# A depthwise convolution as four matmuls on four column groups, fed by four shifted copies made through DRAM

## Chip, core, metric

One Trainium2 chip, one core of it. The metric is the device time of one execution in microseconds (us), as the median of several runs; the profile is of one execution.

## What is computed

A Mamba block and a mixture of experts, both on the layernormed input, both added to it; float32, x of 2 x 2048 rows of 256. What matters here is the convolution of width 4 over time, for each of the 512 inner channels by itself, between a projection and a silu, and the z half beside it:

```python
xn = layernorm(x)
x_in, z = split(xn @ W_in)                    # 512 + 512 columns
conv[d, t] = sum_k conv_w[d, k] * x_in[d, t + k - 3] + conv_b[d]      # zeros ahead of t = 0
u = silu(conv)
dt, B, C = split(u @ W_xproj)                 # 16, 16, 16
delta = softplus(dt @ W_dt + b_dt)
h[t] = exp(delta[t] * A) * h[t-1] + delta[t] * u[t] * B[t]            # 512 channels x 16 states
y[t] = sum_n h[t, n] * C[t, n] + D_skip * u[t]
attn = (y * silu(z)) @ W_out
ffn = sum over the top 2 of 16 experts: w_e * (gelu(layernorm(xn @ W1_e + b1_e)) @ W2_e + b2_e)
out = x + attn + ffn
```

## The kernel before

The 4096 rows are 8 chunks (`c`, `NC`) of 512 time steps. Channels lie on partitions, in four blocks (`dc`) of 128, time along the free axis. A chunk has 64 units (`G = c * 64 + s`, slot `s`), one for each block and state. In a unit ScalarE makes the decay (`exp_unit`, L846, into a ring `hb` of 12), VectorE multiplies du by B (`product`, L1632) and scans (`scan`, L1643), GpSimd multiplies pairs of units by C (`unit_pair`, L658, ring `hc` of 6; for the pairs in `HC_DVE` VectorE does it, `times_c`, L1652), and TensorE adds the states by transposing into `psY` (`sum_unit`, L1150, four units behind).

All else is put between these units by hand-written tables: a table entry names the slot at whose place in an engine's queue the step is issued. `AT` holds for chunks 1 to 6, `AT0` and `AT7` override it for the first and last, `MOE` and `GS` place the twenty groups of the experts, each of four tiles. Each engine walks the same slots; semaphores alone keep them apart. SyncE (SP) issues nearly all loads in the same order, and stands at each wait.

During chunk c, the inputs of chunk c + 1 are made. Every one of these steps passes through one PSUM bank, `psA`, in turn: `project` (two matmuls, L1169), `x_in` (ScalarE copies the bank to `ux`, L780, and three columns for the next chunk's halo, L786), `convolve` (four matmuls of 128 x 128 weights with the diagonal of one tap, `dgw`, on `ux` shifted by the tap, L1177), `x_copy` (bank and bias to `ux`), for dc 3 `x_silu`; then `xd_mm`, `xd_copy`, `d_mm` (L1213), `d_exp`, `d_ln` (`tmpA`, L835) and `d_max` (VectorE, `delta`, L1457). The z half of chunk c takes the same bank in between: `z_mm` (L1225), `z_copy`, `z_silu` (L874 and L876) and, on VectorE, `gate` (L1659). A silu needs another activation table than exp and ln, so `x_silu` and `z_silu` are each followed by a `preload_act_table_set(LNEXP)` (L805, L877), and the compiler puts a load ahead of each activation whose set isn't there.

Ahead of the loop stands a prologue: all rows are normed and transposed (L463, L1324), the router's logits are made on TensorE in four groups of 32 columns (L1339), the routing is worked out on VectorE in one long chain, which needs a matmul over ranks (L1373, behind the convolution of dc 2 in TensorE's queue), and the first chunk's projections, convolutions, x_dbl (L1308) and first delta are made. SP loads x and stores the normed rows and their transpose meanwhile.

## Time and profile before

| | |
|---|---|
| median of 3 runs | 1123.73 us (1122.23 to 1125.07) |
| span of the profiled execution (the only time recorded for it) | 1114.4 us |
| granted TensorE clock, mean | 0.925 |
| busy: VectorE, PE, GpSimd, ScalarE | 1036.3, 930.9, 881.2, 867.0 us |
| moved by DMA | 185.86 MB, 167 GB/s |

The profile's span runs from the first to the last instruction; the median of the runs holds what lies around it as well. PE is TensorE's matmuls, DVE VectorE, ACT ScalarE, POOL GpSimd, SP and SPq SyncE and its queue. L1177 is line 1177 of the kernel.
### The profile page before, as it was taken

The page shows a single profiled execution, that of the slowest core. Times are in us where ns is not written, and L with a number is a line of the kernel's source. Part 1 is how long each engine was busy: PE and PEld are TensorE (multiplying, and loading weights), DVE is VectorE, ACT ScalarE, POOL GpSimd, SP SyncE. Part 2 cuts the span into 40 slices and gives each one's busy share as a digit, 9 for nine tenths or more (in the row PEclk, how much of TensorE's full clock was granted, in tenths as well). Part 3 has the DMA queues.
Part 4 walks back from the last instruction along what each step waited for, and adds up shares of the span by engine and source line. Part 5 has one row for each costly group of instructions (what it writes and reads, how often), then busy time and mean ns, then how long its engine had stood idle before and what let it go on. Part 6 is the DMA issues. An engine that isn't in the chain of part 4 may idle for free.

```text
span 1114.4 us, 16950 instructions
## 1 busy us (share of the span) xinstructions
PE 930.9 (84%) x4575; PEld 630.4 (57%) x4575; DVE 1036.3 (93%) x1304; ACT 867.0 (78%) x1841; POOL 881.2 (79%) x570
## 2 busy tenths in 40 slices
PE   5947766587979999789998999899989999787776
PEld 3424434454656656566666766576656665565564
DVE  7999999799999988997899979999999999899995
ACT  4574788465897799767999699978998798976981
POOL 7178999599777887858787878887897886877995
PEclk9968986698999999899999999799998999899988
DMA  9496568953484544824457553763367443764313
GB/s 328 175 342 227 161 194 290 331 183 92 117 283 153 114 102 143 307 49 95 119 166 278 104 139 75 274 190 72 81 191 266 100 105 92 243 213 114 77 20 66
DMA packets 119367, 185.86 MB, mean 167 GB/s; under 512 B 12012, under 2 KB 104344, under 8 KB 111016
## 3 DMA queue, kind: packets, MB, share of 16 engines
q1 hardware_dynamic: 87120, 144.60, 38.8%
q0 software_dynamic: 19584, 25.26, 13.1%
q10 hardware_dynamic: 12568, 14.93, 4.4%
q8 instruction: 36, 0.59, 0.2%
q14 instruction: 59, 0.48, 0.1%
HBM read 146.34 MB, written 42.60 MB: 170 GB/s over the span
## 4 chain that ended last, share of the span: by engine, by line
PE 36%; issue 16%; ACT 15%; DVE 13%; POOL 11%; DMA 5%; ACTq 2%; SPq 1%; POOLq 0%; DVEq 0%
DVE hb L1643 10%; POOL hc L658 7%; PE psY L1150 7%; PE psA L1177 5%; PE psC L1290 4%; ACT hb L846 4%; PE psC L1240 3%; PE psA L1225 3%; PE psA L1169 2%; PE psE L1267 2%; ACT hnT L967 2%; DVE psB L1632 2%; POOL out L707 2%; DMA Cb<-bc_d 2%; DMA xs_d<-xg,slots 2%
## 5 line engine op out<-in xcount | busy, mean ns | idle before, releaser
L658 POOL TENSOR_TENSOR hc<-hb,Cb 128x1024 f32<-128x1024 f32 x246 | 623.8, 2630 | 83.3 <-PE psY L1150 64.4
L1643 DVE TENSOR_TENSOR_SCAN hb<-hb,carry,psB 128x512 f32<-128x512 f32 x384 | 471.8, 1263 | 7.7 <-ACT hb L846 6.1
L1150 PE MATMUL psY<-ident,hc 128*128 128x128 f32 x2048 | 306.9, 291 | 76.3 <-POOL hc L658 76.2
L846 ACT ACTIVATE hb<-delta,aneg 128x512 f32<-128x512 f32 x512 | 351.5, 716 | 21.7 <-POOL hc L658 15.7
L1150 PEld LDWEIGHTS psY<-ident,hc 128*128 128x128 f32 x2048 | 255.1, 150 | 191.0 <-POOL hc L658 109.4
L1632 DVE TENSOR_TENSOR psB<-Bb,psU 128x512 f32<-128x512 f32 x510 | 323.7, 679 | 0.5 <-DMA Bb<-bc_d 0.5
L707 POOL DMA_INDIRECT out<-yo,idx x80 | 128.0, 1600 | 55.3 <-DMA out<-yo,idx 18.0
L1643 DVE TENSOR_TENSOR_SCAN hb<-hb,psB 128x512 f32<-128x512 f32 x128 | 149.2, 1200 | 2.1 <-ACT hb L846 2.1
L1177 PE MATMUL psA<-ux,dgw 128*128 128x512 f32 x232 | 113.7, 610 | 3.0 <-ACT ux L786 2.0
L1290 PE MATMUL psC<-w2r,hnT 128*128 128x256 f32 x320 | 90.0, 430 | 0.0
L1267 PE MATMUL psE<-w1r,xgT 128*128 128x256 f32 x320 | 82.9, 404 | 0.0
L1290 PEld LDWEIGHTS psC<-w2r,hnT 128*128 128x128 f32 x320 | 63.9, 210 | 18.5 <-issue 10.0
L1267 PEld LDWEIGHTS psE<-w1r,xgT 128*128 128x128 f32 x320 | 59.3, 195 | 16.2 <-issue 9.3
L1169 PE MATMUL psA<-xnT,win 128*128 128x512 f32 x116 | 59.0, 626 | 11.2 <-ACT zs L876 5.0
L967 ACT ACTIVATE hnT<-hnT,vecs 128x128 f32<-128x128 f32 x160 | 64.2, 481 | 1.2 <-issue 0.7
L1225 PE MATMUL psA<-win,xnT 128*128 128x512 f32 x128 | 61.2, 600 | 3.0 <-ACT zs L869 2.2
L1240 PE MATMUL psC<-wout,ygT 128*128 128x256 f32 x248 | 59.8, 383 | 1.2 <-ACT ygT L885 0.8
L1177 PEld LDWEIGHTS psA<-ux,dgw 128*128 128x128 f32 x232 | 41.4, 198 | 31.9 <-issue 26.3
L673 POOL DMA_INDIRECT xs_d<-xg,slots x37 | 40.9, 1104 | 19.2 <-DMA xg<-xn_d 11.4
L1213 PE MATMUL psA<-xr,rows 16*128 16x512 f32 x60 | 40.7, 763 | 15.0 <-DVE delta L1457 14.3
L980 ACT ACTIVATE yo<-psC,wv 128x256 f32<-128x256 f32 x80 | 33.3, 468 | 21.2 <-PE psC L1290 21.2
L666 POOL TENSOR_TENSOR du<-delta,ux 128x512 f32<-128x512 f32 x31 | 44.6, 1438 | 6.6 <-DVE delta L1457 4.4
(235 smaller groups left out, 1205.8 us busy)
## 6 DMA issues: line engine op xcount, KB each, us to landing
Bb<-bc_d SPq DMA_DIRECT2D x32, 1024.0 KB, 6.7
Cb<-bc_d SPq DMA_DIRECT2D x32, 1024.0 KB, 7.5
w1r<-w1c_d SPq DMA_DIRECT2D x80, 256.0 KB, 2.8
w2r<-in_L_ffn_W SPq DMA_DIRECT2D x80, 256.0 KB, 3.5
xg<-xs_d SPq DMA_DIRECT2D x20, 516.0 KB, 5.8
xg<-xn_d SPq DMA_DIRECT2D x37, 128.0 KB, 2.9
Bb<-in_L_attn_x SPq DMA_DIRECT2D x8, 512.0 KB, 7.5
xn_d<-hb SPq DMA_DIRECT2D x8, 512.0 KB, 8.9
```

The source lines that it names most:

```text
L658: pool.tensor_tensor(hc[:, k:k + 2, :], hb[:, g % HR:g % HR + 2, :], Cb[:, n:n + 2, :], ALU.mult).then_inc(s_g, 1)
L707: pool.indirect_dma_start(out=out[:, :], out_offset=bass.IndirectOffsetOnAxis(ap=idx[:, g % 2, j:j + 1], axis=0), in_=yo[:, j, :], in_offs ...
L846: act.activation(hb[:, g % HR, :], delta[:, dc, :], ACT.Exp, scale=aneg[:, dc, n:n + 1]).then_inc(s_exp, 1)
L967: ins = act.activation(hnT[:, j, kc, :], hnT[:, j, kc, :], ACT.Gelu, scale=g1t[:, bass.ds(e, 1), kc], bias=be1t[:, bass.ds(e, 1), kc])
L1150: mm = pe.matmul(y[:, tt * P:(tt + 1) * P], hc[:, g % GR, tt * P:(tt + 1) * P], ident[:, :], start=False, stop=(n == NS - 1), is_transpose ...
L1177: mm = pe.matmul(bank[:, :], dgw[:, dc, k, :], x_of(p, dc)[:, k:k + T], start=(k == 0), stop=(k == KW - 1))
L1225: mm = pe.matmul(psA[:, :], xnT[:, c % 2, kc, tt * P:(tt + 1) * P], win[:, 1, kc, :], start=(kc == 0), stop=(kc == KC - 1))
L1240: mm = pe.matmul(psC[:, 0:D], ygT[:, dc, :], wout[:, dc, :], start=(dc == 0), stop=(dc == dc_out(c) - 1))
L1267: mm = pe.matmul(psE[:, a * D:(a + 1) * D], xgT[:, a, kc, :], w1r[:, a, kc, :], start=False, stop=(kc == KC - 1), skip_group_check=True)
L1290: mm = pe.matmul(psC[:, a * D:(a + 1) * D], hnT[:, 2 * h + a, kc, :], w2r[:, 2 * h + a, kc, :], start=False, stop=(kc == KC - 1), skip_gro ...
L1632: dve.tensor_tensor(psB[g % 2][:, :], Bb[:, n, :], psU[:, :], ALU.mult).then_inc(s_dbu, 1)
L1643: dve.tensor_tensor_scan(h, h, psB[g % 2][:, :], first, ALU.mult, ALU.add).then_inc(s_scan, 1)
```

## The change

The convolution of a block is now made of four matmuls that each have 32 output columns. `ux` of a block is stored to DRAM (`xin_d`, with three halo columns ahead of each sequence), and read back four times, each time shifted by one tap, so that partition 4 c + tap of `xc` holds channel c of 32 at that tap, for four groups of 32 channels side by side. A matmul over 128 partitions (32 channels x 4 taps) with the weights `cwb` gives 32 channels, and the four of them write four partition groups of the bank. The halo copies of ScalarE and the halo columns of `ux` go; `xin_d`'s zero halo is written once by two DMAs. Taps of the first chunk's dc 1 and 3 land in `Cb` and `w2r`, all others in `xc`. The weights' tables are made from one 128 x 32 mask (`near`), and `conv_w` is loaded in rows and transposed with the other vectors. In every chunk, x and z alternate in `psA` block by block (project, x_in, z_mm, z_copy, convolve, x_copy), where they came by halves. The bank's steps now stand ahead of the chunk's and the experts' fills in TensorE's queue, and `z_silu` directly ahead of `x_silu` in the code; its table preload is kept in the last chunk alone. `AT`, `AT0`, `AT7`, `HC_DVE`, `GS` and `MOE` have other numbers. The source of zeros for the experts' empty rows moves into `yo`.

```diff
+CB = P // KW
+NBLK = P // CB
...
-    "x_mm": [5, 5, 8, 9, 9, 10, 18, 18, 21, 21, 21, 23, 28, 28, 31, 32, 32, 32, 34, 34, 37, 37, 37, 37],
-    "x_in": [7, 20, 29, 37],
-    "x_copy": [14, 25, 33],
-    "x_silu": [39],
-    "z_mm": [14, 15, 25, 27],
-    "z_copy": [15, 17, 27],
-    "z_silu": [28],
-    "gate": [30, 45, 54, 3],
...
+AT = {'x_load': [49], 'x_mm': [5, 5, 9, 10, 10, 16, 17, 17, 24, 26, 26, 33], 'x_in': [5, 11, 18, 28], 'x_st': [3, 9, 18, 28], 'x_taps': [3, 11, 18, 29], 'x_copy': [10, 16, 25], 'x_silu': [36], 'xd_mm': [37, 37, 38, 38], 'xd_copy': [40], 'd_mm': [41, 47, 54, 0], 'd_exp': [43, 50, 56, 3], 'd_ln': [44, 51, 61, 3], 'd_max': [49, 54, 63, 3], 'du': [54, 5, 20, 31], 'e_tr': [4, 7, 11, 15], 'e_trc': [5, 11, 13, 15], 'e_mm': [4, 5, 12, 16], 'e_copy': [8, 12, 14, 17], 'z_mm': [5, 13, 19, 29], 'z_copy': [8, 14, 23], 'z_silu': [31], 'gate': [36, 42, 62, 2], 'dskip': [4, 8, 33, 50], 'bc_load': [51, 59, 61, 61], 'carry': [0]}
+AT0 = {'x_load': [36], 'x_mm': [7, 7, 13, 14, 14, 19, 21, 22, 28, 32, 32, 38], 'x_in': [7, 14, 24, 35], 'x_st': [0, 7, 18, 30], 'x_taps': [2, 9, 20, 30], 'x_copy': [14, 24, 33], 'x_silu': [41], 'xd_mm': [39, 40, 41, 43], 'xd_copy': [44], 'd_mm': [43, 45, 57, 6], 'd_exp': [45, 49, 55, 5], 'd_ln': [45, 53, 57, 11], 'd_max': [48, 55, 61, 17], 'd0_exp': [0, 1, 5], 'd0_max': [3, 4, 6], 'du': [55, 0, 11, 36], 'z_mm': [9, 19, 24, 32], 'z_copy': [8, 22, 25], 'z_silu': [39], 'gate': [38, 49, 55, 4], 'dskip': [0, 1, 36, 49], 'bc_load': [50, 52, 59, 61], 'carry': [0]}
...
-HC_DVE = [2, 10, 12, 14, 20, 54, 56, 64, 86, 180]
+HC_DVE = [2, 4, 12, 50, 52, 56, 64, 132, 510]
...
 
         xn_d = dram("xn_d", (NT, D))
+        xin_d = dram("xin_d", (NB, DI, HALO + L))
...
-        dgw = sb("dgw", [P, DC, KW, P])
+        cwb = sb("cwb", [P, DC, NBLK, CB])
+        xc = sb("xc", [P, NBLK, T])
+        near = sb("near", [P, CB])
         wout = sb("wout", [P, DC, D])
...
-
             return ux[:, (c * DC + dc) % UR, :]
+
+        def rep_place(p, dc):
+
+            if p == 0 and dc % 2 == 1:
+                return (1, Cb[:, 0:NBLK, :]) if dc == 1 else (2, w2r[:, :, :, :].rearrange("p a k d -> p a (k d)"))
+            return 0, xc[:, :, :]
+
+        def rep_turn(p, dc):
+
+            return 1 if p == 0 and dc % 2 == 1 else dc // 2 + 1 if p == 0 else 2 + (p - 1) * DC + dc + 1
 
...
                 sp.dma_start(xnT[:, p % 2, :, :], xnT_d[b, :, :, q * T:q * T + T]).then_inc(s_xT, 16)
+
+            def rows_of_x(p, dc):
+                b, q = divmod(p, CPB)
+                return xin_d[b, dc * P:(dc + 1) * P, q * T:q * T + HALO + T]
+
+            def store_x(p, dc):
+                sp.wait_ge(s_xi, p * DC + dc + 1)
+                sp.dma_start(rows_of_x(p, dc)[:, HALO:], u_of(p, dc)).then_inc(s_xd_st[dc], 16)
+
+            def load_taps(p, dc):
+                j = p * DC + dc
+                k, place_x = rep_place(p, dc)
+                if j == 0:
+                    sp.wait_ge(s_halo, 32)
+                sp.wait_ge(s_xd_st[dc], 16 * (p + 1))
+                if k == 0 and j > 0:
+                    sp.wait_ge(s_xp, 1 if p == 0 else j)
+                for tap in range(KW):
+                    sp.dma_start(place_x[tap::KW, :, :],
+                                 rows_of_x(p, dc)[:, tap:tap + T].rearrange("(i c) t -> c i t", c=CB)).then_inc(s_rep[k], 16)
 
             def load_bc(p, q):
                 if q == 0:
...
-            sp.wait_ge(s_cdve, 2)
+            sp.wait_ge(s_cdve, 5)
+            for b in range(NB):
+                sp.dma_start(xin_d[b, :, 0:HALO].rearrange("(c p) h -> p c h", p=P), halo0[:, :, :]).then_inc(s_halo, 16)
...
+                if g == 5:
+                    store_x(0, 0)
+                if g == 6:
+                    load_taps(0, 0)
+            for dc in range(1, DC):
+                store_x(0, dc)
+            for dc in range(1, DC):
+                load_taps(0, dc)
...
                     if c + 1 < NC:
+                        for dc in at(c, "x_st", s):
+                            store_x(c + 1, dc)
+                        for dc in at(c, "x_taps", s):
+                            load_taps(c + 1, dc)
...
-
-                for k in range(h * KW // 2, (h + 1) * KW // 2):
-                    pool.tensor_scalar(dgw[:, dc, k, :], ident[:, :], cw[:, dc, k:k + 1], None, ALU.mult).then_inc(s_wc, 1)
+            def conv_weights(dc):
+
+                for i in range(NBLK):
+                    pool.tensor_scalar(cwb[:, dc, i, :], near[:, :], cwt[:, dc, i:i + 1], None, ALU.mult).then_inc(s_wc, 1)
...
-                    conv_weights((g - 1) // 2, (g - 1) % 2)
-            for h in range(2):
-                conv_weights(DC - 1, h)
+                if g == 3:
+                    pool.wait_ge(s_vec, 1)
+                    pool.wait_ge(s_const, 18)
+                if 3 <= g < 3 + DC:
+                    conv_weights(g - 3)
...
                 act.activation(u_of(p, dc), bank[:, :], ACT.Copy).then_inc(s_xi, 1)
-                if p + 1 < NC:
-                    if j + DC >= UR:
-                        act.wait_ge(s_xp, j + DC - UR + 1)
-                    if p == 0:
-                        act.wait_ge(s_cdve, NCONST)
-                    act.activation(x_of(p + 1, dc)[:, 0:HALO], halo0[:, :] if (p + 1) % CPB == 0 else bank[:, T - HALO:T],
-                                   ACT.Copy).then_inc(s_xi, 1)
...
                 act.activation(zs[:, TT - 1, :], psA[:, :], ACT.Silu).then_inc(s_zc, 1)
-                act.preload_act_table_set(LNEXP)
+                if c == NC - 1:
+                    act.preload_act_table_set(LNEXP)
 
             def y_copy(c, tt):
                 j = c * TT + tt
...
                             carries(G - s % CQ - CQ)
-                    for half in range(2):
+                    for k in range(DC):
                         if c + 1 < NC:
-                            for dc in at(c, "x_in", s, half, half + 1):
-                                x_in(c + 1, dc, psA)
-                            for dc in at(c, "x_copy", s, half, half + 1):
-                                x_copy(c + 1, dc, psA)
-                        for tt in at(c, "z_copy", s, 2 * half, 2 * half + 2):
-                            z_copy(c, tt)
+                            for _ in at(c, "x_in", s, k, k + 1):
+                                x_in(c + 1, k, psA)
+                        for _ in at(c, "z_copy", s, k, k + 1):
+                            z_copy(c, k)
+                        if c + 1 < NC:
+                            for _ in at(c, "x_copy", s, k, k + 1):
+                                x_copy(c + 1, k, psA)
+                    for _ in at(c, "z_silu", s):
+                        z_silu(c)
                     if c + 1 < NC:
-                        for half in range(2, DC):
-                            for dc in at(c, "x_in", s, half, half + 1):
-                                x_in(c + 1, dc, psA)
-                            for dc in at(c, "x_copy", s, half, half + 1):
-                                x_copy(c + 1, dc, psA)
                         for _ in at(c, "x_silu", s):
                             x_silu(c + 1, psA)
                         for _ in at(c, "xd_copy", s):
...
 
-            def convolve(p, dc, k, bank):
-                if k == 0:
-                    pe.wait_ge(s_xi, 2 * (p * DC + dc + 1) if p + 1 < NC else 2 * p * DC + dc + 1)
-                mm = pe.matmul(bank[:, :], dgw[:, dc, k, :], x_of(p, dc)[:, k:k + T], start=(k == 0), stop=(k == KW - 1))
-                if k == KW - 1:
-                    mm.then_inc(s_xp, 1)
+            def convolve(p, dc, bank):
+                k, place_x = rep_place(p, dc)
+                pe.wait_ge(s_rep[k], 16 * KW * rep_turn(p, dc))
+                for i in range(NBLK):
+                    mm = pe.matmul(bank[i * CB:(i + 1) * CB, :], cwb[:, dc, i, :], place_x[:, i, :], start=True, stop=True)
+                mm.then_inc(s_xp, 1)
 
             def x_mm(p, i):
-                dc, j = divmod(i, KC + KW)
+                dc, j = divmod(i, KC + 1)
                 if i == 0 and p == 1:
                     pe.wait_ge(s_te, 4)
                 elif i == 0:
                     pe.wait_ge(s_xT, 16 * (p - 1))
                 if j == 0 and dc == 0:
                     pe.wait_ge(s_delta, p * DC)
-                elif j == 0 and dc == 3:
+                elif j == 0:
                     pe.wait_ge(s_xe, p * DC + dc)
-                elif j == 0:
-                    pe.wait_ge(s_zc, (p - 1) * TT + 2 * dc)
                 if j < KC:
                     project(p, dc, j, psA)
                 else:
-                    convolve(p, dc, j - KC, psA)
+                    pe.wait_ge(s_zc, (p - 1) * TT + dc + 1)
+                    convolve(p, dc, psA)
 
             def xd_mm(p, dc):
                 if dc == 0:
...
             def z_mm(c, tt):
-                if tt % 2 == 1:
-                    pe.wait_ge(s_zc, c * TT + tt)
-                elif c + 1 < NC:
-                    pe.wait_ge(s_xe, (c + 1) * DC + tt // 2 + 1)
+                if c + 1 < NC:
+                    j = (c + 1) * DC + tt
+                    pe.wait_ge(s_xi, j + 1)
...
+            pe.wait_ge(s_wc, DC * NBLK)
             for dc in range(1, DC):
-                for k in range(KW):
-                    convolve(0, dc, k, bank0(dc))
+                convolve(0, dc, bank0(dc))
...
                         d_mm(c, 3)
+                    for k in range(DC):
+                        if c + 1 < NC:
+                            for i in at(c, "x_mm", s, k * (KC + 1), k * (KC + 1) + KC):
+                                x_mm(c + 1, i)
+                        for _ in at(c, "z_mm", s, k, k + 1):
+                            z_mm(c, k)
+                        if c + 1 < NC:
+                            for i in at(c, "x_mm", s, k * (KC + 1) + KC, (k + 1) * (KC + 1)):
+                                x_mm(c + 1, i)
+                    if c + 1 < NC:
+                        for dc in at(c, "xd_mm", s):
+                            xd_mm(c + 1, dc)
+                        for dc in at(c, "d_mm", s, 0, 3):
+                            d_mm(c + 1, dc)
                     for kind, a, b in [v for v in C_TURN if C_FILL[v] == G]:
                         if kind == "y":
                             y_tr(a, b)
...
```

## Rows read from the trace of the kernel before

**Rows 1.** The page's totals: busy time, share of the span and instructions of each engine.

```profile
PE 930.9 (84%) x4575; PEld 630.4 (57%) x4575; DVE 1036.3 (93%) x1304; ACT 867.0 (78%) x1841; POOL 881.2 (79%) x570
```

**Rows 2.** Windows by stage (us, busy us per engine with instructions, granted clock, DMA share, GB/s).

```profile
0.00:62.00 62.00, 48.56 (x279) 25.93 (x279) 52.94 (x172) 31.55 (x69) 26.98 (x47) 0.98 0.72 247
62.00:100.00 38.00, 17.40 (x60) 10.82 (x60) 35.46 (x38) 19.20 (x42) 31.79 (x27) 0.68 0.87 318
100.00:1070.00 970.00, 834.42 (x4090) 569.70 (x4089) 915.75 (x1059) 801.15 (x1704) 790.57 (x484) 0.93 0.56 161
```

**Rows 3.** Waits of VectorE from 100 to 1070 us: us in total, times, longest.

```profile
DVE zs L1659 <- ACT zs L874: 17.0, 5, 7.3
DVE delta L1457 <- ACT tmpA L835: 16.9, 8, 7.6
DVE hb L1643 <- ACT hb L846: 8.2, 10, 2.5
```

**Rows 4.** The chain that ended last, on the page: shares by engine, by line.

```profile
PE 36%; issue 16%; ACT 15%; DVE 13%; POOL 11%; DMA 5%; ACTq 2%; SPq 1%; POOLq 0%; DVEq 0%
DVE hb L1643 10%; POOL hc L658 7%; PE psY L1150 7%; PE psA L1177 5%; PE psC L1290 4%; ACT hb L846 4%; PE psC L1240 3%; PE psA L1225 3%; PE psA L1169 2%; PE psE L1267 2%; ACT hnT L967 2%; DVE psB L1632 2%; POOL out L707 2%; DMA Cb<-bc_d 2%; DMA xs_d<-xg,slots 2%
```

**Rows 5.** Waits of GpSimd, whole span.

```profile
POOL hc L658 <- PE psY L1150: 64.4, 27, 9.0
```

**Rows 6.** Lines by form: busy us, mean ns | idle before.

```profile
L1177 PE MATMUL psA<-ux,dgw 128*128 128x512 f32 x232 | 113.7, 610 | 3.0 <-ACT ux L786 2.0 <-ACT ux L780 1.1
...
L1652 DVE TENSOR_TENSOR hc<-hb,Cb 128x1024 f32<-128x1024 f32 x10 | 16.9, 1691 | 3.8 <-PE psY L1150 3.5
...
L877 ACT ACT_TABLE_LOAD x8 | 10.3, 1283 | 0.1
...
L786 ACT ACTIVATE ux<-psA 128x3 f32<-128x3 f32 x21 | 3.6, 170 | 0.0
...
L1339 PE MATMUL psC<-Cb,wr 128*32 128x128 f32 x48 | 1.9, 279 | 0.0
```

**Rows 7.** Timeline of PE in the prologue: start, us.

```profile
26.50 0.65 PE L1339 MATMUL psC<-Cb,wr 128*32 128x128 f32 x16
...
35.03 1.88 PE L1169 MATMUL psU<-xnT,win 128*128 128x512 f32 x4
...
47.29 0.38 PE L1373 MATMUL psB<-xgT,later 128*128 128x512 bf16 x1
...
47.72 3.60 PE L1177 MATMUL psY<-ux,dgw 128*128 128x512 f32 x8
51.48 3.61 PE L1308 MATMUL psE<-ux,wxd 128*48 128x512 f32 x8 [0.17 <-issue]
```

**Rows 8.** Windows in and just behind the prologue.

```profile
26.00:35.00 9.00, 9.00 (x99) 5.29 (x97) 8.33 (x30) 5.51 (x14) 7.10 (x9) 1.00 1.07 392
...
62.00:66.00 4.00, 0.76 (x1) 0.00 (x0) 4.00 (x6) 4.00 (x11) 3.08 (x4) 0.50 1.00 356
```

**Rows 9.** DMA issues: KB each, median us to landing.

```profile
Bb<-bc_d SPq DMA_DIRECT2D x32, 1024.0 KB, 6.7
...
w1r<-w1c_d SPq DMA_DIRECT2D x80, 256.0 KB, 2.8
...
xn_d<-hb SPq DMA_DIRECT2D x8, 512.0 KB, 8.9
...
w1c_d<-w1r ACTq DMA_DIRECT2D x6, 256.0 KB, 4.5
```

**Rows 10.** Timeline of SyncE's queue: four issues in a row.

```profile
59.64 1.99 SPq L500 DMA_DIRECT2D xg<-xn_d  x4
```

**Rows 11.** The chain in order of time, 0 to 22 us.

```profile
4.37 6.10 DMA Bb<-in_L_attn_x
```

**Rows 12.** Timeline of VectorE in the prologue.

```profile
49.84 1.22 DVE L1568 TENSOR_TENSOR_SCAN yo<-zs,psB 128x512 f32<-128x512 f32 x1
...
59.46 0.74 DVE L1457 SCALAR_TENSOR_TENSOR delta<-psA,vecs,tmpA 128x512 f32<-128x512 f32 x1
```

147 lines of the change are left out of this document (32 added, 115 removed).

## The prediction

> **What bounds the kernel now.** I read the page's totals and then the stages [rows 1, 2]. The main loop of 512 units begins at 62 us, and in it VectorE is the busiest engine, but not by much: from 100 to 1070 us it works 915.75 of 970 us, TensorE 834, ScalarE 801, GpSimd 791. Before the loop comes a prologue of 62 us that is added to the end in full. So there are two accounts to keep: what the prologue gets longer or shorter, and how much of VectorE's idle time in the loop, 970 - 915.75 = 54.25 us, is filled.
>
> The waits of VectorE in the loop say who leaves it idle [rows 3]: 17.0 us before the gate (`zs`, it waits for the silu of z), 16.9 us before the delta (through ScalarE's `tmpA`, which follows TensorE's small matmul) and 8.2 us before scans whose decay is late. The reader is to see that nearly all go back to work that passes through bank `psA` or stands in TensorE's queue. The chain that ended last agrees [rows 4]: PE has 36% of it, VectorE 13%, and the convolution's line alone (L1177) 5%. GpSimd waits 64.4 us for the sums too [rows 5], so it isn't the bound either. TensorE's queue is the thing that makes the others late, in the part of each chunk where projections, convolutions, z and the last chunk's output all stand.
>
> **What the convolution costs on TensorE.** Before: 32 of them, each four matmuls recorded as eight, 3.43 us (from 47.72 us, when the last of the prologue starts, about 3.6 to its modelled end; 113.7 us for 29 of them is 3.9 at a clock that is partly lower) [rows 6, 7]. After: four matmuls of 32 output columns, each on its own column group, over 512 columns. The nearest row is the router's (L1339), four groups of 32 columns over 128 columns: 16 records in 0.65 us with modelled ends [rows 7]. One after another, by the 512-column rate (3.43/8/4 = 0.107 us for a record of 128 columns), they would take 1.7 us; so the groups run side by side, 2.6 times or more. Ideal for the new one is 3.43/4 = 0.86; at 2.6 times it is 1.3. I take 1.1: 2.3 us less for each, 28 in the loop: 65 us less TensorE work. Lower bound of the gain: nothing, if four streams of 512 columns get in each other's way; upper 2.6 x 28 = 72. The Trainium skill ("TensorE: Matmul & The Clock Gate", Part 3) gives 3.07 times for four tiles of this length; by that a convolution would take 1.12 us and the sum would be the same. The same skill ("TensorEngine Tiling (Array Packing)", Key Properties) says that a change of tiling mode drains TensorE, which speaks against: 56 such switches in the loop. The trace shows the router's matmuls following transposes with no gap on record.
>
> **The loop.** I can't read the gain off as 65 us, since only 54 are idle on VectorE, and what is left behind TensorE (ScalarE 83% busy, GpSimd 82%) has waits of its own. L1177 is 5% of the chain [rows 4], 56 us; 4 x 3.43 = 13.7 of it lie in the prologue; of the other 42 us the four groups leave a third, so -28. Filling half of the idle time gives -27. I take **-27**; bounds: 0 and -45 (all but 9 us of it filled).
>
> Three small terms. Pairs of the product with C on VectorE go from 10 to 9 at 1.69 us [rows 6]: **-1.7**; the pair more on GpSimd is covered by its 64.4 us of waits. The last pair (510) is now VectorE's: at the end it follows the last scan at once, and no longer behind an output DMA on GpSimd: **-1**. ScalarE loses 28 halo copies of 0.17 us [rows 6], 5 us, beside other work: 0. "Silus together" saves no table load: in the general table z's silu has slot 31 and x's slot 36, and five units with an exponential stand between. I walked ScalarE's order through both versions: seven loads of 1.28 us [rows 6] at the end of z_silu go, and seven come back ahead of the next exponential or logarithm (none in chunk 2, where a gelu follows, two in chunk 4, where a logarithm follows an exponential that any set serves): 0; cover gone, 9 us over seven places.
>
> **What is added, in the loop.** Each convolution gets a store of 256 KB and four loads of 256 KB, so 1.25 MB, 5 MB in a chunk of some 130 us, 39 GB/s on 161; the DMA share of 0.56 [rows 2] goes to about 0.70. From the end of ScalarE's copy to the last landing: issue 0.5, store 2.8 to 4.5, four issues at 0.5 (1.99 for four), last landing 2.8 more, together 8.1 to 10; at 6.7, the landing of a 1 MB load, up to 13.7 [rows 9, 10]. The general table gives it slots 5 to 9, 11 to 16, 18 to 24 and 28 to 33, at (1070-100)/480 = 2.0 us a unit: 8, 10, 12, 10 us. So it fits, the first one with nothing to spare. The waits that it puts in place: SP stands at each store until the copy is there (x_st 3 for an x_in at 5, 9 for 11) and at each group of taps until the store has landed. Behind it stand the loads of the experts' weights, of `xg`, and of B and C for the next chunk; who waits for them is TensorE at t1, w1 and w2, and VectorE at its product. They have at least three slots, 6 us, and most five or more; I take 0, upper bound in the rival below.
>
> **The prologue gets longer.** (a) Two DMAs of the zero halo, 1,024 pieces of 12 bytes, and a wait for five memsets are put on SP ahead of the third load of x. That load, issued at 4.37 us, is in the chain for 6.1 us [rows 11]. Two issues are 1 us, the pieces I put at 1 more (an 8 KB load of 512 such pieces goes from another queue): **+2**, bounds 1 and 4. (b) The convolution of dc 0 needs its store and four loads while the DMA engines are full (1.07 of their time, 392 GB/s, from 26 to 35 us [rows 8], landings of 8.9 us for stores [rows 9]). SP issues the store at 28, is free at 35.5, has issued the taps at 37.5, and 1 MB at 390 GB/s lands at about 40.5. TensorE stands at that convolution from about 32, and behind it in its queue are the last router transpose and the projections of dc 1 to 3. Those began at 35.03 [rows 7]; now at 41.5, end 46.7. (c) Then the copy (0.6), the third store, and 12 loads at 0.5 us of SP each, or 3 MB at 390 GB/s, 8: the last lands at about 57, its convolution ends at 58, against 51.3. The rank matmul, behind the convolution of dc 2, goes from 47.29 to about 55; VectorE, working without a gap, wants it at 49.84, and its own chain to the first delta at 59.46 [rows 7, 12] is so 5 us late; the other branch, through silu and x_dbl (TensorE 51.48), 6.6 late. The larger counts: **+6.6**. (d) TensorE now stands idle twice for some 8 us before the projections and x_dbl. From 62 to 66 us, after such a lull, the granted clock is 0.50, the lower of its two levels, 1.2 GHz [rows 8]; **+1** for matmuls at half speed. Together **+9.6**, bounds +3 and +15. The Trainium skill ("DMA: Bandwidth & Descriptors", How a descriptor splits into AXI transactions) says that a piece that doesn't start on 256 bytes costs an extra transaction, and the halo shifts every row by 12 bytes and each tap by 4: by that, the taps take nine transactions for eight, an estimate of 0.3 us more for each MB. No row of this trace shows it.
>
> **Sum.** Span 1114.4 + 9.6 - 27 - 1.7 - 1 = 1094.3. The profiled execution has no other time on record than its span; the median of the runs, 1123.73, lies 9.3 above it, and I carry these over: **1103.6, say 1104**. About 0.3% (3.4 us) is what a measurement of this kernel can tell from no change.
>
> **The rivals.**
> - *A, forecast (50%)*: as above; own range 1090 to 1118.
> - *B, the taps come too late (16%), slower*: the conv waits on TensorE for its DMAs, and everything in that queue with it. Place: the first and last convolution of a chunk, behind SP's order. With 13.7 us for the way and 10 given, 3.5 us lateness, 28 times, against 2.3 saved: 34 us more for TensorE, half of it at the end: 1123.7 + 9.6 - 2.7 + 17 = 1148. It decides from a mean lateness of about 1.7 us, where the rest, 0.6 x 28 = 17 at the same 27/65, just pays for the prologue. For: full queues around the loads of B and C, at the seams of the chunks. Against: landings of 2.8 us for 256 KB in the middle of them.
> - *C, TensorE wasn't the bound (12%), slower or same*: ScalarE's or GpSimd's own order leaves VectorE waiting, and only prologue and small terms remain: 1123.7 + 9.6 - 2.7 = 1131. Against: chain and waits, above.
> - *D, more of the idle time goes (14%)*: -45 in the loop, prologue +5: 1123.7 + 5 - 45 - 2.7 = 1081.
> - *E, the clock (5%)*: TensorE with less to do gets more lulls and the lower level. From 0.93 in the loop [rows 2] to 0.86 its remaining 770 us become 63 more, the whole saving: 1131. The Trainium skill ("TensorE: Matmul & The Clock Gate", HAM oscillation) has a matmul loop that falls back in each DMA wait; the 0.68 of 62 to 100 us agrees in kind.
> - *F, the column groups run one after another (3%)*: 3.43 us again, 1131 or more. Against: rows 6 and 7.
>
> Faster: A nearly whole (48), D (14), a little of B and C (4): 0.66. Same: 0.09. Slower: 0.25. The range leaves out the far end of B and a part of D: 1084 to 1135.
>
> **What would show it.** Right: convolution of about 1 us in four concurrent groups; first scan at 70 to 73 us instead of 62; VectorE's idle time in the loop near 27 us; PE's share of the chain down. TensorE's wait on the taps should be near 0 in the loop and some 8 us on the first in the prologue; 40 ScalarE loads for gelu and 33 others as before. Wrong if TensorE waits over 50 us on the taps (B), if VectorE's idle time stays at 50 with TensorE's work 60 us less (C), or if the prologue is no longer than before, which would take 10 us off.

## The result, and the profile after

The changed kernel takes 1249.8 us (median of 4 runs, 1235.7 to 1255.5), the kernel before beside it 1123.0 us. The ratio is 1.111, 95% interval 1.106 to 1.116: 11% slower. The ratio is taken over the fast runs, without the one of 1255.5 us. The forecast was 1104 with a range of 1084 to 1135. The profiled execution has a span of 1247.9 us against 1114.4, so there are 133.5 us to find by spans. By medians they are 127: in every other execution here the time is 1.7 to 1.9 us above the span, so the span of 1114.4 belongs to an execution of about 1116 us, at the quick end of what the kernel before takes in the sets below (1114.9 to 1128.7).

Totals and chain of the changed kernel, from its page:

```profile
PE 907.7 (73%) x4574; PEld 620.6 (50%) x4575; DVE 1042.0 (84%) x1302; ACT 867.1 (69%) x1816; POOL 878.6 (70%) x574
...
PE 25%; ACT 20%; DMA 19%; issue 15%; POOL 9%; DVE 5%; SPq 5%; ACTq 2%; POOLq 0%; DVEq 0%
DMA xc<-xin_d 8%; POOL hc L645 6%; PE psY L1129 5%; ACT hb L828 5%; DMA xin_d<-ux 5%; SPq L445 4%; DVE hb L1618 3%; PE psA L1148 3%; PE psA L1157 3%; DMA xg<-xs_d 3%; PE psC L1217 3%; PE psC L1267 2%; POOL out L695 2%; ACT hnT L950 2%; PE psE L1244 2%
```

No engine has more work than before [rows 1] but for VectorE's 6 us, so the 133 us are waiting. DMA had 5% of the chain [rows 4] and has 19%, of which 13% are the stores of x and the loads of its taps, and the issuing queue 4% more. Windows of the same three stages as in [rows 2]:

```profile
0.00:62.00 62.00, 29.06 (x225) 17.46 (x225) 40.69 (x142) 20.85 (x52) 20.59 (x46) 0.86 0.84 259
62.00:100.00 38.00, 16.87 (x59) 5.67 (x60) 17.35 (x36) 15.24 (x24) 7.61 (x9) 0.59 0.73 165
100.00:1070.00 970.00, 726.24 (x3573) 492.77 (x3574) 826.35 (x949) 705.99 (x1486) 710.33 (x440) 0.86 0.67 189
```

VectorE's idle time from 100 to 1070 us is 144 us, where it was 54. Who ends it has changed as well. Waits of VectorE in that stretch:

```profile
DVE hb L1618 <- ACT hb L828: 98.9, 47, 6.6
DVE zs L1634 <- PE psY L1129: 13.9, 3, 11.6
DVE delta L1432 <- ACT tmpA L817: 12.7, 11, 2.0
```

The silu of z and delta, which led in [rows 3], cost no more than before. New is the wait for exponentials, 98.9 us against 8.2: ScalarE comes to them late. What delays it is in the waits of the whole span, and below them TensorE's for the taps from 100 to 1070 us alone:

```profile
PE psA L1157 <- DMA xc<-xin_d: 84.2, 17, 14.9
ACT ux L774 <- PE psA L1157: 72.5, 15, 15.1
```
```profile
PE psA L1157 <- DMA xc<-xin_d: 69.3, 16, 12.2
```

TensorE stands 84.2 us at convolutions into `psA` whose taps aren't there, 14.9 of them at the prologue's first and 69.3 in the loop (the prologue's other three write other banks and come below). ScalarE stands 72.5 us at the copy of the same convolutions, and the exponentials are queued behind that copy. The lateness isn't spread evenly. The loop in three stretches by time:

```profile
100.00:340.00 240.00, 142.88 (x614) 89.40 (x614) 205.38 (x233) 140.93 (x346) 186.16 (x124) 0.73 0.78 242
340.00:580.00 240.00, 191.79 (x960) 133.99 (x960) 209.95 (x240) 178.83 (x371) 167.55 (x103) 0.89 0.62 175
580.00:1070.00 490.00, 391.56 (x2000) 269.38 (x2000) 411.02 (x477) 386.22 (x770) 356.63 (x215) 0.92 0.63 170
```

Of the 69.3 us, 45 lie before 340 us, where the DMA share is 0.78 and the granted clock 0.73; the six waits behind 700 us that exceed 2 us are of 2.2 to 3.7 us each. One trip in the loop, SyncE's queue (two lines) and then TensorE:

```profile
445.29 0.35 SPq L434 DMA_DIRECT2D xin_d<-ux  x1
448.87 2.54 SPq L445 DMA_DIRECT2D xc<-xin_d  x4
```
```profile
457.66 1.94 PE L1157 MATMUL psA<-xc,cwb 128*32 128x512 f32 x8 [5.58 <-DMA xc<-xin_d]
```

Store to landing 3.6 us, four issues 2.5, last landing 6.2: 12.4 us. The convolution then takes 1.94 us, at a granted clock of 0.50. The prologue, the same two engines:

```profile
40.34 2.58 SPq L445 DMA_DIRECT2D xc<-xin_d  x4
...
60.32 2.53 SPq L445 DMA_DIRECT2D Cb<-xin_d  x4
62.95 5.80 SPq L445 DMA_DIRECT2D xc<-xin_d  x4
68.80 6.72 SPq L445 DMA_DIRECT2D w2r<-xin_d  x4
```
```profile
50.48 1.94 PE L1157 MATMUL psA<-xc,cwb 128*32 128x512 f32 x8 [14.90 <-DMA xc<-xin_d]
...
70.55 1.93 PE L1157 MATMUL psU<-Cb,cwb 128*32 128x512 f32 x8 [11.25 <-DMA Cb<-xin_d]
77.44 1.94 PE L1157 MATMUL psC<-xc,cwb 128*32 128x512 f32 x8 [4.96 <-DMA xc<-xin_d]
...
81.99 1.94 PE L1157 MATMUL psY<-w2r,cwb 128*32 128x512 f32 x8 [1.64 <-DMA w2r<-xin_d]
```

From 60.3 us twelve loads bring 3 MB, and the last convolution starts at 82.0: 21.7 us, some 145 GB/s. A window inside it (us, busy us per engine, granted clock, DMA share, GB/s):

```profile
63.00:69.00 6.00, 0.00 (x0) 0.00 (x0) 0.13 (x1) 0.00 (x0) 0.00 (x0) 0.50 1.00 134
```

The DMA engines are busy the whole time and move 134 GB/s, where a share of 1.07 moved 392 before [rows 8]. The first scan starts at 95.32 us instead of 62.17.

### The profile page after: what moved, and what is told of

Read it like the earlier page. It is cut to its first block, busy times and chain, and to the rows that moved or that the text cites. A ratio compares the mean times of both kernels' runs of the same rounds, so it can differ in the third digit from the quotient of the medians.

```text
span 1247.9 us, 17145 instructions
## 1 busy us (share of the span) xinstructions
PE 907.7 (73%) x4574; PEld 620.6 (50%) x4575; DVE 1042.0 (84%) x1302; ACT 867.1 (69%) x1816; POOL 878.6 (70%) x574
## 4 chain that ended last, share of the span: by engine, by line
PE 25%; ACT 20%; DMA 19%; issue 15%; POOL 9%; DVE 5%; SPq 5%; ACTq 2%; POOLq 0%; DVEq 0%
DMA xc<-xin_d 8%; POOL hc L645 6%; PE psY L1129 5%; ACT hb L828 5%; DMA xin_d<-ux 5%; SPq L445 4%; DVE hb L1618 3%; PE psA L1148 3%; PE psA L1157 3%; DMA xg<-xs_d 3%; PE psC L1217 3%; PE psC L1267 2%; POOL out L695 2%; ACT hnT L950 2%; PE psE L1244 2%
## 5 line engine op out<-in xcount | busy, mean ns | idle before, releaser
L1129 PE MATMUL psY<-ident,hc 128*128 128x128 f32 x2048 | 319.5, 299 | 66.8 <-POOL hc L645 64.3
L1129 PEld LDWEIGHTS psY<-ident,hc 128*128 128x128 f32 x2048 | 266.8, 155 | 147.3 <-POOL hc L645 84.9
L1157 PE MATMUL psA<-xc,cwb 128*32 128x512 f32 x232 | 42.8, 819 | 84.3 <-DMA xc<-xin_d 84.2
L1244 PE MATMUL psE<-w1r,xgT 128*128 128x256 f32 x320 | 89.4, 415 | 0.0
L1148 PE MATMUL psA<-xnT,win 128*128 128x512 f32 x116 | 65.2, 688 | 11.4 <-DVE delta L1432 10.9
L1217 PE MATMUL psC<-wout,ygT 128*128 128x256 f32 x248 | 65.8, 411 | 7.9 <-ACT ygT L868 5.9
L774 ACT ACTIVATE ux<-psA,vecs 128x512 f32<-128x512 f32 x22 | 15.1, 686 | 77.4 <-PE psA L1157 72.5
L1226 PE MATMUL psC<-ident,xg 128*128 128x128 f32 x160 | 28.3, 305 | 49.8 <-DMA xg<-xs_d 25.1
L1217 PEld LDWEIGHTS psC<-wout,ygT 128*128 128x128 f32 x248 | 48.0, 202 | 26.2 <-ACT ygT L868 9.7
L769 ACT ACTIVATE ux<-psA 128x512 f32<-128x512 f32 x29 | 17.3, 597 | 51.4 <-PE psA L1148 46.9
```

Source lines behind the costliest of these rows:

```text
L1129: mm = pe.matmul(y[:, tt * P:(tt + 1) * P], hc[:, g % GR, tt * P:(tt + 1) * P], ident[:, :], start=False, stop=(n == NS - 1), is_transpose ...
L1148: mm = pe.matmul(bank[:, :], win[:, 0, kc, dc * P:(dc + 1) * P], xnT[:, p % 2, kc, :], start=(kc == 0), stop=(kc == KC - 1))
L1157: mm = pe.matmul(bank[i * CB:(i + 1) * CB, :], cwb[:, dc, i, :], place_x[:, i, :], start=True, stop=True)
L1217: mm = pe.matmul(psC[:, 0:D], ygT[:, dc, :], wout[:, dc, :], start=(dc == 0), stop=(dc == dc_out(c) - 1))
L1244: mm = pe.matmul(psE[:, a * D:(a + 1) * D], xgT[:, a, kc, :], w1r[:, a, kc, :], start=False, stop=(kc == KC - 1), skip_group_check=True)
```

## The experiments

All spans are of one profiled execution each; the kernel before was run beside every set. Two kinds of difference are read: one of spans, and ratios of several rounds, which have intervals. Spans of one kernel in one set lie up to 15 us apart (the kernel before 1113.1 to 1124.4, p0_first 1156.2 to 1171.0), so a difference of two single spans under some 12 us is not read as an effect.

**1. The transfers alone.** A kernel with only the taps' loads in several forms, three times over, each waited for before the next.

> Measures transfers alone: nothing of the block is computed, x is only copied to the output. Each form moves 1 MB (four loads of 256 KB, each waited for as a group), three times, with nothing else in flight; one form at a time differs from the changed kernel's: rows of DRAM that start on 256 bytes, with or without the shift between the taps; 32 neighbouring partitions as destination in place of every fourth; one load of 1 MB; the shift made on the side of SBUF; a copy within SBUF; a store to shifted or unshifted rows. Theory A (the start of the rows in DRAM makes the loads slow): the changed kernel's form takes 7 us or more for 1 MB, as in its prologue, and the forms with even starts 4 to 5 us whatever their partitions. Theory B (every fourth partition makes them slow): the even start doesn't help and the neighbouring partitions do. Theory C (the loads are only slow beside other traffic): all forms take about 4.5 to 5 us here.

SyncE's queue, second time over; the time of a form is the distance to the next line. The mark `...` stands for one form, the shift made on the side of SBUF (g), issued at 118.68:

```profile
86.00 2.60 SPq L44 DMA_DIRECT2D a_after<-src_odd  x4
93.40 2.52 SPq L44 DMA_DIRECT2D b_even<-src_even  x4
99.38 1.75 SPq L44 DMA_DIRECT2D c_contig<-src_odd  x4
106.75 1.73 SPq L44 DMA_DIRECT2D d_both<-src_even  x4
113.70 0.38 SPq L44 DMA_DIRECT2D e_one<-src_even  x1
...
125.53 2.52 SPq L44 DMA_DIRECT2D h_oddpitch<-src_even  x4
131.57 10.44 SPq L44 DMA_DIRECT2D i_sbuf<-ux  x16
143.43 0.34 SPq L44 DMA_DIRECT2D src_odd<-ux  x1
146.39 0.33 SPq L44 DMA_DIRECT2D src_even<-ux  x1
148.42 1.96 SPq L44 DMA_DIRECT2D a_after<-src_odd  x3
```

As in the changed kernel (rows 8204 bytes apart) 1 MB takes 7.40 us; with rows 8448 bytes apart, which keeps all of them on 256 bytes, 5.98; with that pitch and starts 12 to 24 bytes past such a multiple (h) 6.04. Neighbouring partitions instead of every fourth save issue time (1.75 against 2.6 us), and nothing in total: 7.37 us with the odd pitch, and 6.95 with the even one, a full microsecond more than every fourth. Form g moves 1.13 MB in 6.85 us, about 6.1 per MB. A store of 256 KB takes 2.96 us to rows of odd pitch and 2.03 to even ones. Copies inside SBUF (i) take 11.9, of which 10.4 are SyncE's sixteen issues. So with every fourth partition, as in the kernel, the pitch costs 1.4 us per MB and 0.9 per store; the shift doesn't. Theory A had the shifted start and the pitch as one thing, and 4 to 5 us for all even forms: it is right on the odd form's 7 us alone.

**2. From the changed kernel down.** Three variants. Without any trip, no call of `store_x` or `load_taps`, and the column groups on the unshifted x:

```
-                pe.wait_ge(s_rep[k], 16 * KW * rep_turn(p, dc))
+                pe.wait_ge(s_xi, p * DC + dc + 1)
...
-                    mm = pe.matmul(bank[i * CB:(i + 1) * CB, :], cwb[:, dc, i, :], place_x[:, i, :], start=True, stop=True)
+                    mm = pe.matmul(bank[i * CB:(i + 1) * CB, :], cwb[:, dc, i, :], u_of(p, dc), start=True, stop=True)
```

> Leaves out the way through DRAM (no store, no taps are loaded; the four matmuls read the unshifted x from SBUF, so the shift of the convolution is left out); all slots, the order of the queues and the column groups stay. Theory 1 (the way through DRAM costs all of the loss and more): about 1085 to 1105 us, first scan near 60 us after the start, VectorE's idle time in the loop well under 54 us. Theory 2 (the new slots and the new order in bank psA cost a large part): 1150 us or more, with the waits for the decay (ACT hb) still there.

With all transfers and SyncE's waits for them, but TensorE reading `u_of` as above. Since TensorE no longer guards the buffers, other engines do: SyncE also waits for the taps before it overwrites them and before the first loads of B and C, and ScalarE for the store before its copy:

```
+                    sp.wait_ge(s_rep[0], 16 * KW * (rep_turn(p, dc) - 1))
...
+            sp.wait_ge(s_rep[1], 64)
+            sp.wait_ge(s_rep[2], 64)
...
+                act.wait_ge(s_xd_st[dc], 16 * (p + 1))
```

> Keeps every store and every load of the taps and all waits of SyncE for them, but the four matmuls read the unshifted x from SBUF (so the shift is left out) and TensorE waits for no load. The copy that overwrites x waits for the store. Theory 1a (TensorE's wait for the taps is the cost): near the run without the way, at most 15 us above it. Theory 1b (SyncE's queue, blocked at stores, makes the other loads late, or the traffic does): within 40 us of the changed kernel, 1210 or more, with TensorE waiting for the experts' weights and rows.

With rows of even pitch (`ROW0` is 64) and all four taps loaded from the unshifted start:

```
-        xin_d = dram("xin_d", (NB, DI, HALO + L))
+        xin_d = dram("xin_d", (NB, DI, ROW0 + L))
...
-                                 rows_of_x(p, dc)[:, tap:tap + T].rearrange("(i c) t -> c i t", c=CB)).then_inc(s_rep[k], 16)
+                                 rows_of_x(p, dc)[:, ROW0:ROW0 + T].rearrange("(i c) t -> c i t", c=CB)).then_inc(s_rep[k], 16)
```

> The changed kernel, except that a row of the DRAM copy has 64 columns ahead in place of 3, so that stores and loads start on 256 bytes, and all four taps load the same unshifted columns (so the shift is left out). Theory A (start of the rows): the loads take about 4.5 us for 1 MB and not 7, the prologue is some 10 us shorter, and the time falls to 1170 to 1200. Theory B or C: within 10 us of 1250.

Measured: spans 1155.0, 1183.7 and 1187.4 us. n1_notrip is Theory 2: even without the trip the kernel is 40 us slower than before, which neither account of the forecast has. n2_unread lies 29 us above it, between its two theories; 9.6 us of that is one wait of VectorE for B right after the first scans, and ScalarE's added waits for the stores are 13.0 us. So only the whole of the trip, n1 to the changed kernel, is priced cleanly (93 us), and the split between traffic and TensorE's waits is rough. a1_aligned is in Theory A's range. The waits of n1_notrip from 100 to 1070 us:

```profile
DVE hb L1605 <- ACT hb L816: 47.7, 33, 5.5
...
ACT ux L757 <- PE psA L1136: 39.3, 18, 5.2
...
ACT xgT L870 <- PE psC L1213: 28.5, 13, 9.4
```

**3. Is TensorE's relief worth anything, and whose are the 40 us?** The kernel before with four column groups on the unshifted x, all else as it was; they are issued once, at `k == KW - 1`:

```
-                mm = pe.matmul(bank[:, :], dgw[:, dc, k, :], x_of(p, dc)[:, k:k + T], start=(k == 0), stop=(k == KW - 1))
...
+                if k < KW - 1:
+                    return
...
+                for i in range(4):
+                    mm = pe.matmul(bank[32 * i:32 * i + 32, :], dgw[:, dc, i, 32 * i:32 * i + 32], x_of(p, dc)[:, HALO:], start=True, stop=True)
```

> The kernel before, with its tables and queues, where the four 128-column matmuls of a convolution become four of 32 columns on four column groups, issued at the slot of the last of the four; they read the unshifted x, so the shift and three of the taps are left out. TensorE's work falls by 65 to 75 us, nothing else changes. Theory 1 (what the prediction took: TensorE's relief fills half of VectorE's idle time): about 1090 us, first scan at about 55. Theory 2 (the relief is worth nothing, since the engines wait for each other's slots and not for TensorE's work): 1110 to 1125.

The variant without the trip, with `GS` and `MOE` of before:

> The run without the way through DRAM (shift left out, as there), with the experts' tables GS and MOE of the kernel before; all else as in that run (1156.85 us). Theory M (the experts' new slots cost the 40 us): 1120 to 1130. Theory L (ScalarE's copies of bank psA stand in the very slot of TensorE's matmul, and ScalarE waits there): within 10 us of 1157.

The variant without the trip, with ScalarE's copies in `AT` two slots or more behind their matmuls (`x_mm` 5, 5, 9, 12, ...; `x_in` 7, 14, 21, 28):

> The run without the way through DRAM (shift left out, as there), but in the general table each copy of bank psA by ScalarE stands two slots behind the matmul that fills it, as in the kernel before (x_in 7, 14, 21, 28 for projections at 5, 12, 19, 26; z_copy and x_copy two slots behind theirs); the first and last chunk's tables are left. Theory L: the waits of VectorE for the decay (ACT hb, 48 us) fall to 20 or less, the time to 1125 to 1140. Theory M: within 8 us of 1157.

Measured: n3_groups 1117.2 us, beside 1120.4 of the kernel before on that chip; span 1115.5. Its line of the convolution, and its window in the loop:

```profile
L1179 PE MATMUL psA<-ux,dgw 128*32 128x512 f32 x232 | 34.2, 664 | 0.4 <-ACT ux L786 0.4
```
```profile
100.00:1070.00 970.00, 796.40 (x4102) 548.31 (x4101) 916.96 (x1062) 799.02 (x1703) 790.80 (x484) 0.91 0.56 161
```

The convolution falls from 113.7 to 34.2 us, TensorE's work in the window by 38 us (its clock is 0.91 instead of 0.93), and VectorE gets 1.2 us more done [rows 2]. So Theory 2 holds: TensorE's relief of 38 us brings no gain that one run can tell from scatter, and the 27 us of the forecast are excluded. n4_oldmoe and l1_lag came out at spans of 1189.1 and 1173.2, both worse than the 1155.0 they start from and outside the ranges of both their theories; in l1_lag VectorE's wait for exponentials grows from 47.7 to 65.1 us, where Theory L had it at 20 or less. Neither idea holds.

**4. Can the trip be made cheap?** The whole convolution with the even pitch; x stands from element 64 of a row, its halo in 61 to 63:

```
+                                 rows_of_x(p, dc)[:, ROW0 - HALO + tap:ROW0 - HALO + tap + T].rearrange("(i c) t -> c i t", c=CB)).then_inc(s_rep[k], 16)
```

> The changed kernel with one thing moved: the rows of x in DRAM are 2112 elements long instead of 2051 and x begins at element 64 of each, so that every row and every store begins on a multiple of 256 bytes, and only the loads of taps begin 12, 8, 4 or 0 bytes before one. It computes the whole convolution. Theory R (what costs in the trip is the odd pitch, which gives every row another offset; a shifted start costs nothing: 6.1 against 7.4 us per MB in the measurement of the forms): as good as the variant whose taps are not shifted at all, span 1185 to 1195. Theory S (the shift of the three taps costs as much as the pitch): half way or less, 1215 to 1248.

The same, with chunk 0 convolved from SBUF:

> The kernel with the even pitch, and chunk 0 convolved from SBUF without its trip through DRAM: its stores and loads of taps are gone and its four column groups read the unshifted copy (left out: the shifts of chunk 0's taps, and chunk 1's first three columns see zeros). First scan at 64 us, as in the variant without any trip. If what the prologue loses passes whole to the end, the span falls by 18 (82 less 64) against the even pitch, to about 1170; if the loop takes some of it up again, it falls by under 9. Against the variant without any trip (1155.0) what remains is then the loop's trip alone: 15 us if the prologue passes whole.

And from the variant without the trip, all other work's slots back to those of before:

> The variant without the trip, with every table that isn't the projections', the convolution's, x_dbl's and delta's own taken from the kernel before: slots of the experts, group starts, the transposes' and projection's of y, du, gate, skip, the loads of B and C, carries, and VectorE's pairs. Theory P (the 40 us of the new order lie in the other work's slots, chosen for a kernel that has the trip): back to 1115 to 1130. Theory W (they lie in the weave of x and z itself, with its copies in the same slots as their matmuls): 1150 or more, ScalarE still waiting some 60 us on psA. The variant that took only the experts' slots back came out at 1189, so a mix may also be worse than either, which would speak for slots that only work as a set.

Measured: a2_pitch 1178.3 us, ratio 1.051 (1.045 to 1.057), span 1177.8, first scan at 80.4 us. That is 70 us better than the changed kernel for one number in the layout, and no worse than the unshifted a1 (1187.4): Theory R holds, with a span a little under its range. The twelve loads of the prologue now take 12.2 us instead of 21.7, and a window among them moves 310 GB/s at a lower DMA share (same columns as above):

```profile
58.00:64.00 6.00, 1.93 (x8) 0.23 (x8) 0.13 (x1) 0.04 (x1) 0.00 (x0) 0.50 0.91 310
```

Its wait for taps, whole span (31.8 us of it in the loop):

```profile
PE psA L1158 <- DMA xc<-xin_d: 41.9, 8, 11.8
```

p0_first 1164.4 us, ratio 1.037 (1.032 to 1.042), first scan at 65.4: the first scan comes 15.0 us earlier, and the time falls by 13.9 us by the medians. The profiled spans differ by 6.8 only (1177.8 and 1171.0, the longest of its four), so that the prologue passes whole to the end is likely and not shown. s4_rest_of_before came out at a span of 1194.5: P falls, and W isn't shown by it, since n4 too was worse than both kernels it is mixed from.

**5. Do the exponentials need more lead?** One number, seven slots instead of six, without the trip and as a control in the kernel before (with the carries of one or two tables at slot 0, which this needs):

```
-LEAD = 6
+LEAD = 7
```

> The variant without the trip, with the exponentials of A issued seven slots ahead of their scan instead of six (the carries of the last chunk move to slot 0 of each four with it). Theory X (the new slots make ScalarE late with the exponentials at times by up to 5 us, and nothing else is lost; one slot of 2 us more would cover a good part of VectorE's 48 us): 1155 span goes to 1120 to 1140, and VectorE's wait for them falls to 15 to 30 us. Theory T (TensorE, ScalarE and GpSimd wait for each other round a ring, and the exponentials are late because the ring is slow): 1150 to 1160, the wait goes elsewhere or stays.

> The control: the kernel before with the same lead of seven slots. Its VectorE waits 8 us for exponentials, so by both theories 1110 to 1122, no difference that counts.

> The variant without the trip, with only the slots of the transposes of y and of the output projection (16 numbers) taken from the kernel before. Theory Y (these, one to three slots earlier or later in the stretch where x and z are woven, cause the waits of ScalarE and TensorE on psC): 1115 to 1140. Theory W (the weave of x and z): 1150 to 1165.

Measured: t_lead7 1161.5 us, ratio 1.034 (1.031 to 1.037); v_lead7 1.002 (0.999 to 1.005); r3_e_slots 1160.3 us. In t_lead7 VectorE's wait for exponentials falls to 36.5 us and that for delta grows from 17.6 to 26.7; the time stays. X and Y fall. The wait went elsewhere and the time stayed, as T has it, though T's ring of waits itself isn't shown: the lateness is passed on from somewhere else.

**6. From the kernel before up.** First only TensorE's order in a slot, on n3_groups: the block with the projections, convolutions, z, `xd_mm` and `d_mm` moves ahead of the loop over `C_TURN` (transposes of y, output projection, the experts' transposes and second matmul). The diff of the change has this move; no step of the prediction costed it.

```
                     for _ in at(c, "d_mm", s, 3):
                         d_mm(c, 3)
-                    for kind, a, b in [v for v in C_TURN if C_FILL[v] == G]:
...
                     for half in range(2):
...
                             d_mm(c + 1, dc)
+                    for kind, a, b in [v for v in C_TURN if C_FILL[v] == G]:
```

> The kernel before with its convolution on column groups (unshifted, as n3_groups), and TensorE's program in a slot in the order of the changed kernel: projections, x_dbl and delta ahead of the work on psC instead of behind it. Theory W (the 40 us come with the weave of x and z and its slots): 1110 to 1125. Theory O (they come with this order: psC's work, on which ScalarE waits, stands behind projections): 1140 or more.

Then the slots of y, du, gate, skip and bc_load in `AT`, then `MOE`, from the changed kernel:

> The same as w5_order, and in the main table the slots of y's transposes and output projection, du, gate, skip and the loads of B and C as in the changed kernel; the projections', convolution's, x_dbl's and delta's slots stay those of before. Theory W: within 10 us of w5_order. Theory P (the other work's slots hold the loss): 1140 or more.

> The same as w6_rest, and the experts' offsets as in the changed kernel (the groups' starts stay). Theory W: within 10 us of w6_rest. Theory P: 1140 or more. If each of the three steps adds 5 to 15 us, the loss belongs to no one part: each set of slots fits only its own kernel.

Measured: spans 1144.6, 1171.4 and 1180.7 us, from 1115.5. The order costs 29, which is Theory O. The first foreign slots cost 27 more; the experts' offsets 9, which a single span can't tell from nothing. The first two steps are larger than the 5 to 15 us of the third expectation, so its split into equal small parts falls.

**7. The order by itself.** The same move in the kernel before, whole, and w5_order timed again:

> The kernel before, whole, with one block of TensorE's program in each slot moved: projections, convolution, x_dbl and delta ahead of the work on psC. Theory O (the order itself: ScalarE stands at its copies of psC, named early in its slot, while TensorE first does up to 4 us of projections and convolution): 1145 to 1160, more than with column groups since the convolution that now stands ahead is 2.3 us longer each. Theory M (the old slots were timed for the long convolution, and only the shortened one meets them badly): 1115 to 1130.

> The kernel of w5_order once more, timed: 1141 to 1152, ratio 1.017 to 1.025 to the kernel before.

Measured: y1_order 1159.6 us, ratio 1.034 (1.028 to 1.040), span 1159.7; w5_again 1151.3 us, ratio 1.025 (1.018 to 1.031). Theory O: the order costs 38 us by the medians with the long convolution, and 29 and 34 by the two spans with the short one. All four times of w5_again (1143.2 to 1152.9) lie under all four of y1_order (1157.1 to 1164.4), so in that order the column groups do gain, some 8 us. Waits of ScalarE from 100 to 1070 us, first in the kernel before, then in y1_order (n3_groups has 36.1 and 14.7, w5_order 66.9 and 29.1):

```profile
ACT om L893 <- PE psC L1240: 36.2, 24, 3.6
...
ACT ygT L885 <- PE psC L1233: 13.7, 14, 2.5
```
```profile
ACT om L893 <- PE psC L1240: 66.4, 21, 5.4
ACT ygT L885 <- PE psC L1233: 27.9, 12, 3.3
```

And one such wait in y1_order, ScalarE, TensorE and VectorE:

```profile
529.33 0.39 ACT L893 ACTIVATE om<-psC 128x256 f32<-128x256 f32 x1 [3.80 <-PE psC L1240]
```
```profile
525.58 1.98 PE L1225 MATMUL psA<-win,xnT 128*128 128x512 f32 x4 [1.35 <-ACT zs L869]
527.40 1.89 PE L1240 MATMUL psC<-wout,ygT 128*128 128x256 f32 x8
```
```profile
531.79 2.45 DVE L1643 TENSOR_TENSOR_SCAN hb<-hb,carry,psB 128x512 f32<-128x512 f32 x2 [4.16 <-ACT hb L846]
```

ScalarE is idle from 525.5 us, at the copy of an output projection that TensorE starts at 527.4, because a projection of z now stands ahead of it, with a wait of its own for ScalarE's last copy. Behind that copy and two more stands the next exponential, at 530.95, and VectorE's scan has waited 4.16 us for it. VectorE's waits for exponentials are 34.1 us in y1_order against 8.2 [rows 3].

These waits don't carry over to the changed kernel as they are. Without the trip, n1_notrip has 18.3 us at `om` and 13.7 at `ygT`, less than or the same as the kernel before; its ScalarE stands at the projection's copy instead (39.3 us against 7.6) and at the experts' `xgT` (28.5 against 1.4). So the order is priced in the old slots alone.

## Why the prediction was wrong, step by step

Four steps failed, in the order of what they cost: the trip in the loop, put at 0, cost 62 us; order and slots, without a term, 40; the loop's gain of 27 didn't come; and the prologue's 9.6 were 33. The table has the spans.

| | span | first scan | from there to the end |
|---|---|---|---|
| before | 1114.4 | 62.2 | 1052.2 |
| n3_groups: column groups | 1115.5 | 64.0 | 1051.5 |
| n1_notrip: and the new order, weave and slots | 1155.0 | 64.3 | 1090.7 |
| n2_unread: and the transfers, not waited for by TensorE | 1183.7 | 72.2 | 1111.5 |
| after: and TensorE waits for the taps | 1247.9 | 95.3 | 1152.6 |
| a2_pitch: after, even pitch | 1177.8 | 80.4 | 1097.4 |
| p0_first: a2, chunk 0 without the trip | 1171.0 | 65.4 | 1105.6 |

- *The convolution on column groups, 1.1 us*: right. A full-clock one is recorded with 1.06 us and the next instruction starts 1.00 after it (at 438.87 us), 3.4 times less than 3.43, which is such a distance of starts. The Trainium skill ("TensorE: Matmul & The Clock Gate", Part 3) has 3.07 times for four row tiles; its row for columns is of three tiles. The other page of the Trainium skill, "TensorEngine Tiling (Array Packing)", Key Properties, has a drain at a change of mode; no gap is on record: at 457.66 us the next transpose starts 1.87 us after a convolution of 1.94. Ends are modelled, so a short drain isn't excluded. The 65 us less work for TensorE were 38 from 100 to 1070 us in n3_groups, and 49 in the span.
- *The loop, -27*: fell. It measured +1 by spans (n3_groups), -3 by single times, near the 0 that was the lower bound of that gain. The step that failed is "L1177 is 5% of the chain, the four groups leave a third, so -28". A share of the chain isn't a price: VectorE's waits for silu and delta stayed. This was rival C, at 12%.
- *TensorE's order in a slot*: no term, no bound, no rival. It costs 38 us alone, in the old slots (y1_order), and is a part of the change that the prediction didn't see. The prediction read what each slot holds and when, and not in which order TensorE does what one slot holds.
- *The rest of the new slots*: no term either. In n1_notrip order, weave and slots together cost 40. How much of the 40 is the order's in the new slots stays open: ScalarE's waits in n1_notrip are others than in y1_order, and no run has the variant without the trip in the old order, or the new group starts in the old kernel. No mix of the two sets was better than the kernel it started from; n4, s4 and w6 were worse by 27 to 40 us, r3 and x3 by no more than the scatter.
- *The trip in the loop, 0*: fell, the largest of the four. The way was put at 8.1 to 10 us, up to 13.7, from landings of rows that lie together; one early trip measured 12.4, against a gap of 8 to 12 us. The mis-sized term is the last landing: 4.8 us behind the last issue on quiet queues (7.40 less 2.60) and 6.2 in the loop, where 2.8 was taken. This is rival B's mechanism: 69.3 us of waits in the loop alone, against its mark of 50. Its place was wrong, for the waits bunch in the first two chunks and not at the first and last convolution of every chunk. Its price came out larger: 62 us in the loop (the changed kernel against n1_notrip, each from its first scan), where B had 17. By n2_unread some 21 of them are traffic and the other waits, 9.6 of these right behind the prologue, and some 41 TensorE's own waits: of TensorE's lateness 41 of 69.3 us arrive, where B took half. ScalarE stands at the same convolution, with the exponentials behind it.
- *The prologue, +9.6*: it was +33.1. (a) right: the third group of x loads is issued at 6.07 us instead of 4.37, +1.7 for 2. (b) the first convolution starts at 50.5 for 40.5: SyncE stands 7.1 us until the store has landed before it can issue the taps, and these land 7.6 us after the last issue. (c) the last convolution starts at 82.0 for 57: 3 MB at 145 GB/s where 390 was taken. This is the prologue's largest error. The rank matmul between them starts near 79.7 for 55, and VectorE stands 17.3 us for it. (d) right in kind: every convolution of the prologue takes 1.94 us, at the lower clock.
- *Even pitch*: the prediction had the rule of the Trainium skill ("DMA: Bandwidth & Descriptors", How a descriptor splits into AXI transactions), an extra transaction for a piece that doesn't start on 256 bytes, and worked out 0.3 us per MB from it, outside of the sum. The runs show no such cost for the start: shifted by 12 to 24 bytes it takes 6.04 against 5.98 us per MB. An odd pitch takes 7.40. The whole price of the pitch in the kernel is 70 us by spans, 55 of it in the loop.
- *Small terms*: seven table loads go and ten come back (the three lines below), 3.8 us more on ScalarE where 0 was put. The walk missed three: in three chunks a logarithm and the exponential behind it (L892, L894) each get a load. The last pair on VectorE, put at -1, takes 4.37 us, and from the last scan to the end of the span it is 17.6 us where it was 14.3. The DMA share of the loop came out at 0.67 for 0.70. About 0.3% as what a measurement can tell was too fine: the kernel before alone ranges over 1% in one set.
- *E, the clock*: 0.86 in the loop, as that rival had it. It isn't the groups' doing, for n3_groups has 0.91; it is lowest, 0.73, in the stretch where TensorE waits for the taps. What the clock itself costs there no run separates from the waits.

```profile
L828 ACT ACT_TABLE_LOAD x4 | 5.1, 1283 | 0.1
L892 ACT ACT_TABLE_LOAD x3 | 3.8, 1283 | 0.1
L894 ACT ACT_TABLE_LOAD x3 | 3.8, 1283 | 0.1
```

By spans the account is: column groups +1, order, weave and slots +40, the trip +93 (31 in the prologue and 62 behind it), together 133.5; the spans' scatter goes into each. No version beat the kernel before: with the even pitch the change is 5% slower, and n3_groups, which computes less, is level with it.
